# A graph network on one core: the usual path in one block, x2 stored by tile block, the last message step written out

## The reference

```python
deg = max(segment_sum(ones, dst), 1); d = deg ** -0.5
h = relu(layernorm(x))
feat = h                                   # layer 0: 10 hops
for i in range(10):
    agg = segment_sum(feat[src] * (d[dst] * d[src])[:, None], dst)
    feat = (0.9 * agg + 0.1 * h) * r[i] + (1 - r[i]) * feat
x = x + feat                               # called x2 below
emb = relu(layernorm(x))                   # layer 1: 4 message steps
for _ in range(4):
    m = (emb @ W_msg.T + b_msg).reshape(n, 4, 128)
    q = segment_sum(m[src, edge_type], dst)
    emb = gru_cell(q, emb)                 # gates r, z, n from q and emb
return x + emb
```

## Time and profile before

| | us |
|---|---|
| median of 3 runs (2457.24 to 2459.94) | 2458.39 |
| the profiled execution | 2458.51 |
| its span, first to last instruction | 2456.7 |
| PE busy | 2162.5 (88%) |
| DVE busy | 1385.1 (56%) |
| ACT busy | 509.4 (21%) |
| mean granted clock of PE | 0.922 |

### The profile page before, as it was taken

How to read it: one execution, slowest core, us unless ns; L and a number is a source line. 1 busy time by engine, 2 the same in 40 slices (tenths; PEclk the granted TensorE clock), 3 DMA queues, 4 the chain that set the end, 5 groups by cost and what they waited for, 6 DMA issues and landing times.

```text
span 2456.7 us, 40725 instructions
## 1 busy us (share of the span) xinstructions
PE 2162.5 (88%) x14377; PEld 1408.0 (57%) x14888; DVE 1385.1 (56%) x2702; ACT 509.4 (21%) x1123; POOL 235.5 (10%) x517
## 2 busy tenths in 40 slices
PE   4545554599999999999799999999999999999996
PEld 2223222489998989898444565444654446544464
DVE  8878787687777777777722337323363224632243
ACT  4868778300000000000400103100031000210010
POOL 4646555000000000000000000000000000000000
PEclk9656656599999999999899999999999999999998
DMA  2000000100000000005100000000000000000001
GB/s 76 22 33 22 29 26 22 50 2 1 2 1 3 1 2 2 2 2 148 48 1 1 1 1 1 1 1 1 1 1 1 1 1 1 1 1 1 1 1 52
DMA packets 21916, 34.30 MB, mean 14 GB/s; under 512 B 2183, under 2 KB 18174, under 8 KB 21201
## 3 DMA queue, kind: packets, MB, share of 16 engines
q1 hardware_dynamic: 18757, 30.56, 3.6%
q10 hardware_dynamic: 2944, 0.93, 0.2%
HBM read 18.04 MB, written 13.45 MB: 13 GB/s over the span
## 4 chain that ended last, share of the span: by engine, by line
PE 77%; DVE 9%; ACT 6%; issue 3%; ACTq 1%; DVEq 1%; DMA 1%; POOL 0%; POOLq 0%
PE ps L855 43%; PE ps L774 27%; PE ps L807 4%; ACT weighed L517 3%; PE ps L795 2%; ACT packed L510 2%; ACTq L490 1%; DVE marks L1041 1%; ACT words L499 1%; DVE dig L1069 1%; DVE big L1071 1%; PE ps L671 1%; DVEq L1028 1%; PE ps L715 1%; DMA x_after_hops<-x 1%
## 5 line engine op out<-in xcount | busy, mean ns | idle before, releaser
L855 PE MATMUL ps<-slots,m_parts 125*128 125x500 fp8e4 (+1 forms) x5600 | 1084.0, 353 | 1.4 <-DVE slots L1341 1.0
L855 PEld LDWEIGHTS ps<-slots,m_parts 125*128 125x128 f16 x5600 | 546.8, 98 | 487.9 <-issue 0.8
L774 PE MATMUL ps<-parts,big 125*128 125x256 f16 x6125 | 669.5, 273 | 6.1 <-DVEq L1388 3.7
L774 PEld LDWEIGHTS ps<-parts,big 125*128 125x128 fp8e4 x6125 | 591.3, 98 | 63.5
L1341 DVE TENSOR_SCALAR slots<-big 128x3200 int32<-128x3200 int32 (+1 forms) x112 | 244.1, 2183 | 280.5 <-PE ps L855 280.4
L671 PE MATMUL ps<-hot_pair,weighed 125*128 125x228 f16 x1000 | 206.4, 351 | 184.3 <-DVE hot_pair L1043 93.8
L671 PEld LDWEIGHTS ps<-hot_pair,weighed 125*128 125x128 f16 x1000 | 111.5, 118 | 279.2 <-ACT weighed L517 242.6
L517 ACT ACTIVATE weighed<-marks,win_w 125x128 f16<-125x128 f16 x625 | 195.6, 390 | 90.0 <-DVE marks L1041 89.0
L456 ACT ACTIVATE rs<-rs 125x25 f32<-125x25 f32 x3 | 0.7, 225 | 717.7 <-DVE rs L920 717.7
L1443 DVE SCALAR_TENSOR_TENSOR r_parts<-ps,over,r_parts 128x500 f16<-128x500 f32 (+1 forms) x28 | 19.1, 683 | 230.1 <-ACT r_parts L587 230.1
L1450 DVE SCALAR_TENSOR_TENSOR gate_r<-ps,over,gate_r 128x500 f32<-128x500 f32 (+1 forms) x28 | 19.1, 682 | 228.6 <-PE ps L807 228.6
(11 more groups left out here) (204 smaller groups left out, 1337.7 us busy)
## 6 DMA issues: line engine op xcount, KB each, us to landing
packed_counts<-packed SPq DMA_DIRECT2D x16, 625.0 KB, 2.9
big<-packed_counts SPq DMA_DIRECT2D x4, 1600.0 KB, 7.5
big<-packed_counts SPq DMA_DIRECT2D x3, 1200.0 KB, 6.5
hd<-in_x SPq DMA_DIRECT2D x1, 1562.5 KB
x_again<-in_x SPq DMA_DIRECT2D x1, 1562.5 KB
x_after_hops<-x SPq DMA_DIRECT2D x1, 1562.5 KB
big<-x_after_hops SPq DMA_DIRECT2D x1, 1562.5 KB
out<-big SPq DMA_DIRECT2D x4, 250.0 KB
```

The lines of the kernel that those rows point to most:

```text
L774: last = pe.matmul(ps[:, n % RING, 0:2 * F], tot_f8[0:Q, c, a, :], both((parts0, parts1)[par], a), start=a == 0, stop=a == TILES - 1)
L855: last = pe.matmul(ps[:, k % 2, 0:SIZES[k] * Q], m_parts[0:Q, a, h, t * F:(t + 1) * F], slots_f8[0:Q, t % 2, 0:SIZES[k], a, 0:Q], start=a ...
```

## The change

1. **One block per path.** On PE, ACT and DVE everything from the flag to the end stands in one `If(over_any < 1)`, and the general path's code in one `If(over_any > 0)` behind it. On SP the general block stands first.
2. **The last message step is written out.** The loop runs over three steps, without conditions inside; the fourth follows as code of its own.
3. **Results leave during it.** PE transposes blocks 0 to 2 between the second and third type of the last block's gathers, 3 and 4 ahead of the last gates, 5 behind them, 6 at the end, into other banks (`OUT_BANK`). DVE's additions stand between its operations. x2 is loaded back from the first block of the last step on.
4. **x2 is stored per tile block** as DVE finishes it in the last hop. Each store, the load back and each store of results is split into rows 0 to 111 and 112 to 124. DVE waits for the stores only after messages 0 to 3.
5. **Roots in three batches**, columns 0 to 15, 16 to 21, 22 to 24 (`NORMED`): the first two batches are normalised within the last hop. `update_scales` moves from tile 3 of the last hop to tile 3 of the one before; the first two unpackings move from tile 17 to tiles 9 and 12. The embedding is read from banks 5, 6, 7, 0, 1, 2, 3 (`EMB_BANK`), and ACT waits until DVE has read the last hop's banks.
6. DVE makes the low halves of two embedding blocks, then messages 0 to 3, then the other five.

Nothing in the arithmetic changes. The core of the diff:

```diff
+NORMED = [(0, 16), (16, 22), (22, 25)]
+EMB_BANK = [5, 6, 7, 0, 1, 2, 3]
+OUT_BANK = [6, 7, 1, 6, 7, 1, 0]
+ROWS_A = 112
...
+            def store_x2(k):
+                a, z = START[k] * F, (START[k] + SIZES[k]) * F
+                sp.wait_ge(s_x2, k + 1)
+                for lo, hi in ((0, ROWS_A), (ROWS_A, Q)):
+                    sp.dma_start(x2_dram[lo:hi, a:z], x2[lo:hi, :, :].rearrange("p c f -> p (c f)")[:, a:z]).then_inc(s_x2_out, 16)
...
-            sp.wait_ge(s_x2, 1)
-            sp.dma_start(x2_dram, x2[0:Q, :, :].rearrange("p c f -> p (c f)")).then_inc(s_x2_out, 16)
-            sp.wait_ge(s_x2_out, 16)
...
+                    store_x2(k)
+                sp.wait_ge(s_slot, TYPES * (BLOCKS * (STEPS - 1) + 1))
+                load_x2()
+                store_results()
...
+            def embed(hops_done=None):
+                for n, (lo, hi) in enumerate(NORMED):
+                    root(3 + n, lo, hi)
+                if hops_done:
+                    act.wait_ge(s_ring, hops_done)
...
+                        if t == 1 and k == BLOCKS - 1 and not more_steps:
+                            for done in range(3):
+                                pe.wait_ge(s_emb, BLOCKS * STEPS + done + 1)
+                                out_transposes(done)
...
+                    for done in (3, 4):
+                        pe.wait_ge(s_emb, BLOCKS * STEPS + done + 1)
+                        pe.wait_ge(s_res, done - 2)
+                        out_transposes(done)
+                    block_gates(BLOCKS - 1)
+                    pe.wait_ge(s_emb, BLOCKS * STEPS + 6)
+                    pe.wait_ge(s_res, 3)
+                    out_transposes(5)
+                    pe.wait_ge(s_emb, BLOCKS * (STEPS + 1))
+                    out_transposes(BLOCKS - 1)
...
+                pe.wait_ge(s_emb, 3)
+                for a in range(AHEAD):
+                    message_when_ready(0, a)
+                with pe.Fori(0, STEPS - 1) as s:
+                    gnn_step(s, True)
+                gnn_step(STEPS - 1, False)
...
-                hop(HOPS - 2, 0, TILES * (HOPS - 2))
+                hop(HOPS - 2, 0, TILES * (HOPS - 2), 3)
...
-                    if c == 3:
-                        update_scales(step)
-                    if c == 17:
-                        unpack(0, 0, 0)
-                        unpack(0, 0, 1)
+                    if c + 1 == START[BLOCK_OF[c]] + SIZES[BLOCK_OF[c]]:
+                        dve.sem_inc(s_x2, 1)
+                    for n, (lo, hi) in enumerate(NORMED):
+                        if c + 1 == hi:
+                            norm_root(n)
+                        if c == hi:
+                            norm_factor(step, n)
+                    if c in (9, 12):
+                        unpack(0, 0, (9, 12).index(c))
+                    if 17 <= c < 21:
+                        norm_tiles(4 * (c - 17), 4 * (c - 16))
+                    if c >= 23:
+                        norm_tiles(16 + 3 * (c - 23), 19 + 3 * (c - 23))
+                norm_factor(step, 2)
+                norm_tiles(*NORMED[2])
...
-            dve.wait_ge(s_x2_out, 16)
...
+                for k in range(2):
+                    first_low(k)
+                messages(0, 0, AHEAD)
+                for k in range(2, BLOCKS):
+                    first_low(k)
+                dve.wait_ge(s_x2_out, 32 * BLOCKS)
```

More of the change, by code:

```diff
@@ new lines, in out_transposes, with message @@
+            def out_transposes(k):
+                for j in range(SIZES[k]):
+                    last = pe.transpose(ps[0:Q, OUT_BANK[k], j * F:(j + 1) * F], emb[:, START[k] + j, :], ident[:, :])
+                last.then_inc(s_otr, 1)
+            def message(s, a):
+                pe.wait_ge(s_mfull, TILES * s + max(a, 1))
+                for n, (h, w) in enumerate(((0, 0), (0, 1), (1, 0))):
+                    last = pe.matmul(ps[0:Q, 6 + a % 2, :], emb_parts[:, h, a, :], w_parts[:, w, :], start=n == 0, stop=n == 2)
+                last.then_inc(s_m, 1)
@@ new lines, in message_when_ready, with gates, product, r @@
+            def message_when_ready(s, a):
+                pe.wait_ge(s_el, BLOCKS * s + BLOCK_OF[a] + 1)
+                message(s, a)
+            def gates(turn, n, bank, e):
+                pe.wait_ge(s_rl, turn + 2)
+                pe.wait_ge(s_sig, 2 * turn + 1)
+                pe.wait_ge(s_ct, turn + 1)
+                def product(out, j, value, start, stop):
+                    for m, (h, w) in enumerate(((0, 0), (0, 1), (1, 0))):
+                        last = pe.matmul(out, g_parts[:, w, j * F:(j + 1) * F], value(h), start=start and m == 0, stop=stop and m == 2)
+                    return last
+                def r(h):
+                    return r_parts[:, bank, h, 0:n]
+                for j in range(2):
+                    product(ps[:, 2 + j, 0:n], 3 + j, e, True, False)
+                    last = product(ps[:, 2 + j, 0:n], j, r, False, True)
+                last.then_inc(s_grz, 1)
+                product(ps[:, 4, 0:n], 2, r, True, True)
+                product(ps[:, 5, 0:n], 5, e, True, True).then_inc(s_gn, 1)
@@ new lines, in gather @@
+            def gather(s, k, ts, a):
+                for t in ts:
+                    for h in range(2):
+                        last = pe.matmul(ps[:, k % 2, 0:SIZES[k] * Q], m_parts[0:Q, a, h, t * F:(t + 1) * F],
+                                         slots_f8[0:Q, t % 2, 0:SIZES[k], a, 0:Q],
+                                         start=a == 0 and t == 0 and h == 0,
+                                         stop=a == TILES - 1 and t == TYPES - 1 and h == 1)
+                    if a == TILES - 1:
+                        last.then_inc(s_slot_free, 1)
@@ L798, in gates @@
-            def gates(turn, n, bank, e):
-                pe.wait_ge(s_rl, turn + 2)
-                pe.wait_ge(s_sig, 2 * turn + 1)
-                pe.wait_ge(s_ct, turn + 1)
-                def product(out, j, value, start, stop):
-                    for m, (h, w) in enumerate(((0, 0), (0, 1), (1, 0))):
-                        last = pe.matmul(out, g_parts[:, w, j * F:(j + 1) * F], value(h), start=start and m == 0, stop=stop and m == 2)
-                    return last
-                def r(h):
-                    return r_parts[:, bank, h, 0:n]
-                for j in range(2):
-                    product(ps[:, 2 + j, 0:n], 3 + j, e, True, False)
-                    last = product(ps[:, 2 + j, 0:n], j, r, False, True)
-                last.then_inc(s_grz, 1)
-                product(ps[:, 4, 0:n], 2, r, True, True)
-                product(ps[:, 5, 0:n], 5, e, True, True).then_inc(s_gn, 1)
@@ L899, in _ @@
[L899 to L902 removed]
+                for k in range(BLOCKS):
+                    if k >= 3:
+                        pe.wait_ge(s_res, k - 2)
+                    out_transposes(k)
         @block.vector
@@ new lines, in norm_tiles, with norm_root, norm_factor @@
+            def norm_tiles(lo, hi):
+                for c in range(lo, hi):
+                    TS(normed[0:Q, c, :], x2[0:Q, c, :], stats[0:Q, c, 0:1], dis[0:Q, c:c + 1],
+                       ALU.subtract, ALU.mult).then_inc(s_nrm, 1)
+            def norm_root(n):
+                lo, hi = NORMED[n]
+                root_of(stats[0:Q, lo:hi, 1], EPS, lo, hi)
+            def norm_factor(step, n):
+                lo, hi = NORMED[n]
+                one_over_root(step, dis[0:Q, lo:hi], 3 + n, lo, hi)
@@ new lines, in _ @@
+            with dve.If(over_any < 1):
+                first_factors(step)
+                first_features(step)
+                hops_fast()
+                steps = Chain(dve, s_dve_late)
+                for k in range(2):
[4 more added lines that the diff above has]
+                dve.wait_ge(s_x2_out, 32 * BLOCKS)
+                for k in range(BLOCKS):
+                    dve.wait_ge(s_pblk[k], 16)
+                with dve.Fori(0, STEPS - 1) as s:
+                    steps.loop(s, 4 * BLOCKS)
+                    gnn_step(s, True)
+                steps.done(STEPS - 1)
+                gnn_step(STEPS - 1, False)
```

428 lines of the change are left out of this document (216 added, 212 removed).

## The result

| | before | after |
|---|---|---|
| median, us | 2457.81 (2455.40 to 2459.94, 4 runs) | 2424.85 (2423.78 to 2427.44, 4 runs) |
| span of the profiled execution, us | 2456.7 | 2423.3 |
| mean granted clock of PE | 0.922 | 0.927 |

The ratio is 0.9868, 95% interval 0.9851 to 0.9885: 33 us faster, where 29.5 were forecast. In the page of the changed kernel, busy times and the instruction queue answer to the earlier trace rows. PE executes the same 14377 matmuls; it is busy 5.5 us less (2157.0 against 2162.5) and idle some 28 us less.

A forecast was written before the change was run, and what follows sets the result against it. The prediction took TensorE (PE), busy 88% of the span, as the bound, with time won where it idles on the path. From 2458.5 us, terms -6.1 +0.4 -11.7 -0.2 +1.5 -13.4 = -29.5 gave 2429.0, range 2423 to 2437.

The forecast's parts named there:

- C: Last hop's last matmul (H) to message 6: no store wait, normalisation mostly inside the hop; -11.7 us, bounds -8 to -12.5.
- A: At the flag: PE takes no jump over general blocks, so the opening pass starts sooner; -6.1 us.
- B: Update of scales moved into the hop before: PE's 0.34 us idle there grows; +0.4 us, bounds 0 to +2.
- D: Message steps: three fewer conditional blocks per step; -0.2 us, bounds 0 and -2.
- E: Last block's gathers: twelve transposes of blocks 0 to 2 run between them on PE's path; +1.5 us.
- F: End: only three transposes, one addition and two stores follow the last embedding, PE's jump closing the span; -13.4 us.
- 1: At the flag: PE's idling is no jump, so the flag keeps its price; 2435.1 us, chance 0.08.
- 4: Last step written out starves for instructions, making the kernel slower than before; 2473 us, chance 0.02.
- 2: End bound by something slower, a store's landing or a longer jump: 5 us more, 2434 us; chance 0.09.
- rival 3: First messages after the hops stay slow, PE kept at half clock: 4 us lost, 2433 us; chance 0.11.
- 5: Last hop: DVE falls behind and PE stalls there, 3 us at most; no separate chance given.

The follow-up runs named there:

- e10: Changed kernel with PE's blocks cut and placed as in the kernel before, counting and general hops ahead of the usual path; 2434.03 us, ratio 0.9902.
- e3: Changed kernel with the update of scales back behind tile 3 of the last hop; 2430.42 us, ratio 0.9887.
- e9: e8 with the first three message steps also written out on PE, ACT and DVE; 2419.80 us, ratio 0.9841.
- e4: Changed kernel, last step still written out, with all 25 transposes, seven additions and fourteen stores behind the last embedding; 2432.17 us, ratio 0.9886.
- e8: Changed kernel with the loop over pairs of hops written out on PE and DVE; 2419.81 us, ratio 0.9844.
- e5: Changed kernel with x2's stores and load and the result stores over 125 rows in one transfer each, not split; 2427.19 us, ratio 0.9882.
- e6: Changed kernel with one root over all 25 tiles and all normalising behind the last hop; 2431.13 us, ratio 0.9893.
- e7: Changed kernel with x2 stored in one 125-row transfer and DVE waiting for it ahead of the first low halves; 2439.81 us, ratio 0.9934.
- e1: Changed kernel with PE's general path ahead of the usual one, in two blocks: the counting, and the rest; 2428.08 us, ratio 0.9871.
- e2: Changed kernel with one more unexecuted PE block, holding a single wait, directly ahead of the usual path; 2423.80 us, ratio 0.9862.
- e11: e9 with low halves of blocks 2 to 6 between first-step messages and result 5 added during the last candidate; 2416.19 us, ratio 0.9824.

## Why the prediction was right

The forecast was 2429.0 with a range of 2423 to 2437; 2424.85 lies in it, 4.2 us below. Of these, 3.9 are seen in the spans (-33.4 against -29.5): 2.7 of them are term C, 0.8 lie ahead of the flag, and the other terms nearly cancel.

- **A, the flag** (-6.1; measured -5.9, good to some 0.8). Right in size and cause: e10 puts both jumps back and gets 5.9 us back. The prediction names the rule that only a far target costs, but its sum prices every jump alike. It didn't matter, since both jumps were far.
- **Ahead of the flag** (0; -0.8). No code differs there. The flag's value comes between 464.6 and 466.3 in the traces shown, so this is the spread of executions and no gain of the change.
- **B, the scales** (+0.4; +0.3, and +0.7 over all of the hops). The one idle in the ninth hop is there, ahead of the matmuls at 1049.68, 0.61 us where 0.34 stood in the kernel before; it was put at 0.8:

```profile
1049.68 25.50 PE L898 MATMUL ps<-parts,big 125*128 125x256 f16 x232 [0.61 <-DVEq L1469]
```

  The other 0.4 of the hops are PE's idles at the three jumps back, 5.7 us against 5.3, which the move doesn't touch. As a term by itself B was right; that it is what makes 3.0 us of C possible (e3), the forecast did not say.
- **C, from the hops to the gathers** (-11.7; -14.4, outside this term's own bounds of -8 to -12.5). The mechanism was right, the size was off, and the step that failed is "its table load, 1.28 us and hidden before under the wait for the store, is now on the path". The row above has ACT's first high half directly behind the last embedding. With it the chain of the forecast becomes: last embedding H + 8.5 (forecast 9.0), first high half done H + 8.9 (10.9), five low halves from H + 13.1 (15.2), the bias of tile 4 from H + 15.6 (17.9), message 6 at H + 16.4 (18.9). 1.3 of the 2.5 us are the table load, 0.5 ACT's earlier end, 0.7 overlaps of a few tenths between neighbouring instructions. The Trainium skill has the rule that I should have applied (ScalarE activation tables: per-element evaluation and per-set limits, Table sets in the compiler and the runtime): table loads are placed block by block. In the kernel before the messages began a block of their own behind a conditional; now embedding and first high halves lie in one block, and the load stands at the head of the loop over steps. The trace agrees: the load is at 1174.20, directly ahead of the loop's first high half, and again at the next step (1486.87); the kernel before had one ahead of the first high half of all (1180.37) and one more at the loop's (1195.85), and e9, where the loop is written out, has none at either place.
- **D and E** (-0.2 and +1.5; -0.7 and +1.3). Both right within 0.5 us, E shown by e4, D as what remains of the difference. The twelve transposes take 1.31 us from row to row, 0.11 each.
- **F, the end** (-13.4; -13.5). Right as a sum, but partly by luck. The forecast let PE's jump over the general block close the span, 5.2 us after the last embedding, with the store's landing ahead of it at 4.5. The jump took 3.4 us by its record and not 3.9 to 5, and was through at 2421.8, 3.6 us after the last embedding. The last store was issued 3.2 us after it (forecast 2.5), and its landing, the later one, closed the span at 5.1. One size too large and one too small met in the right number.
- **The rivals.** 1 and 4 fell by e10 and e8. 2 did not come, though e5 shows its mechanism at 1.9 us. 3 did not come in the profiled run (see the windows below). 5, DVE late in the last hop, came only with the scales back in it (e3), and then at its 3 us, behind the hop and not in it.

One part of rival 3 is open. Windows of the run after and of e10, in which nothing differs but PE's order of blocks, show the granted clock behind message 6 (the figure before the last two):

```profile
1178.00:1190.00 12.00, 11.88 (x56) 6.63 (x65) 10.85 (x18) 5.64 (x9) 0.00 (x0) 1.00 0.00 1
```

```profile
1180.00:1190.00 10.00, 7.34 (x29) 3.62 (x32) 8.57 (x15) 3.88 (x6) 0.00 (x0) 0.83 0.00 0
```

It stays at 2.4 GHz in one and falls for a while to 1.2 in the other, after the same messages and the same 2.6 us of idling: 1.4 us between message 6 and gather 12. e3, e4, e6 and e7 fell too (1.4 to 1.7 us), e1, e2, e5, e8 and e9 did not. In e3 the clock fell in the seventh hop too, and behind changes of steps it fell twice in e1 and once each in e3 and e6, where gather 12 to the last embedding is 0.7 to 2.7 us longer than in the run after. What decides it was not tried; e11, which has no such idle at message 6, kept the clock there.

## What to carry to other kernels

Put the path that runs directly behind its branch: on PE each jump over hundreds of instructions or more took 3.3 to 5.6 us by its record. A loop pays for each jump back too, but less: the records say 3.3 to 3.9 us in the hops, and writing them out won 2.1 each. Where another engine is waited for at that place, it is nothing (e9). When a wait of 10 us is removed, compute what stands second and third behind it, for those decide the gain: here the early roots were worth 4.9 us with the store out of the way and nothing with it. And where work is moved into an engine's free time, move what already stands there first; its cost seen by itself (0.4 us) tells nothing of the 3 us that it makes room for.

## What the runs showed that was not expected

- A taken jump over a few instructions, or over the counting of the general path (a loop body of 32 matmuls), costs 0.32 us; over 125 matmuls more, 3.4 to 3.9; over 250, 5.5 to 5.6; over the whole rest of the general path, 4.8; over all of it, at the end of the program, 3.3 to 3.9. Beyond the first, it isn't the length that is paid for.
- The same kernel with 3,750 more matmuls written out moved fewer packets of instructions (117 against 123) and lost no time to them.
- SP's issue of the first 13-row store behind the last embedding took 1.3 us in the run after, 1.8 in e9, 0.85 in e11 and 0.4 in e1 by its record, and 0.4 where it followed others at once. It is a cost of the split into 112 and 13 rows: in e5, without the split, the last issue ends 1.6 us after the last embedding and not 3.2. It explains only a part of how the end varies, from 4.6 to 6.3 us with the same code there: in e9 and e3, with the longest, 0.4 to 0.5 us more go by until the last issue than in the run after, and 0.8 more pass between the last issue and the end of the span (2.6 and 2.7 us against 1.8). What makes the landing slower there is open.
